# Second projection in one bank of 512 columns, its scores as row products on VectorE, the two score rows in their right roles, and a new order of work

## The reference, cut to what matters

```python
xl = (x @ W).reshape(B, N, H, F)
asrc = jnp.einsum('bnhf,hf->bnh', xl, a_src)
adst = jnp.einsum('bnhf,hf->bnh', xl, a_dst)
e = jax.nn.leaky_relu(asrc[:, :, None, :] + adst[:, None, :, :], NEG_SLOPE)
e = jnp.where(mask[..., None], e, NEG_INF)
attn = jax.nn.softmax(e, axis=1)
out = jnp.einsum('bsdh,bshf->bdhf', attn, xl)
h = jax.nn.elu(gat_layer(x, mask, W1, att_src1, att_dst1, b1, concat=True))
h = gat_layer(h, mask, W2, att_src2, att_dst2, b2, concat=False)
```

## Time and profile before

| | us |
|---|---|
| median of 3 runs (3081.1 to 3087.44) | 3084.61 |
| the profiled execution, its own time | 3083.84 |
| its span, first to last instruction | 3082.1 |
| TensorE busy | 2976.9 (97%) |
| VectorE busy | 2480.0 (80%) |
| ScalarE busy | 2319.9 (75%) |
| GpSimd busy | 2263.2 (73%) |

### The profile page before, as it was taken

The page is one execution under the profiler, slowest core; times in us unless marked ns, Lnnn a source line. Parts: engine busy times, 40 slices in busy tenths (PEclk is TensorE's granted clock), DMA queues, the critical chain, the costliest instruction groups (busy, mean ns, idle before and its releaser), DMA issues. The chain is left out here.

```text
span 3082.1 us, 79166 instructions
## 1 busy us (share of the span) xinstructions
PE 2976.9 (97%) x21040; PEld 2746.1 (89%) x21040; DVE 2480.0 (80%) x8101; ACT 2319.9 (75%) x6433; POOL 2263.2 (73%) x3214
## 2 busy tenths in 40 slices
PE   7899999999999999999999999999999999999974
PEld 5789999999999999999999999999999999999964
DVE  3578888888888888888888888888888888888852
ACT  2567787778877788777787778877788777787752
POOL 3467777777777777777777777777777777777753
PEclk6999999999999999999999999999999999999985
DMA  5123333333333333333333333333333333333332
GB/s 195 34 69 123 117 119 122 108 124 118 119 123 106 125 117 119 122 109 122 118 119 121 108 122 120 120 118 112 121 120 119 118 110 122 120 120 119 96 107 93
DMA packets 205558, 355.71 MB, mean 115 GB/s; under 512 B 51904, under 2 KB 117568, under 8 KB 188736
## 3 DMA queue, kind: packets, MB, share of 16 engines
q1 hardware_dynamic: 205120, 350.66, 34.8%
HBM read 314.93 MB, written 35.59 MB: 114 GB/s over the span
## 5 line engine op out<-in xcount | busy, mean ns | idle before, releaser
L1454 POOL TENSOR_SCALAR rs<-mv,rs 128x1 f32<-128x1 f32 x512 | 357.6, 698 | 109.2 <-POOL rs L1451 108.8
L997 ACT ACTIVATE eT<-eT,tc 128x128 f32<-128x128 f32 x1024 | 314.1, 389 | 161.3 <-POOL eT L1534 161.3
L432 PE MATMUL bank_b<-w_hi,hT_hi 128*128 128x344 f32 x1536 | 419.8, 328 | 5.6 <-DVE g L1277 3.8
L432 PE MATMUL bank_c<-w_hi,g_hi 128*128 128x258 f32 x2048 | 414.1, 283 | 4.7 <-DVE x L1204 4.7
L432 PE MATMUL bank_c<-w_lo,g_hi 128*128 128x258 f32 x2048 | 414.5, 284 | 0.0
L432 PE MATMUL bank_b<-w_lo,hT_hi 128*128 128x344 f32 x1536 | 408.2, 320 | 0.0
L1329 DVE CUSTOM_DVE_ANT_0 t_all_L<-t_all_L,mask 128x128 f32<-128x128 f32 x1024 | 368.6, 413 | 27.0 <-DMA t_all_L<-t_dram_L 26.5
L432 PE MATMUL bank_b<-w_hi,hT_lo 128*128 128x344 f32 x1536 | 357.0, 327 | 0.0
L432 PE MATMUL bank_c<-w_hi,g_lo 128*128 128x258 f32 x2048 | 351.8, 284 | 0.0
L432 PE MATMUL bank_e<-w_hi,hT_hi 128*128 128x264 f32 x1024 | 341.1, 347 | 5.5 <-DVE out_sb L1372 5.4
L1540 POOL TENSOR_TENSOR eT<-eT,shift_all 128x512 f32<-128x512 f32 x256 | 331.1, 1294 | 4.6 <-ACT eT L997 4.4
(11 more groups left out here) (158 smaller groups left out, 8577.5 us busy)
## 6 DMA issues: line engine op xcount, KB each, us to landing
shift_all<-shift_dram SPq DMA_DIRECT2D x128, 1024.0 KB, 5.3
t_all_L<-t_dram_L SPq DMA_DIRECT2D x128, 512.0 KB, 3.7
x_in<-in_x SPq DMA_DIRECT2D x128, 256.0 KB, 2.6
t_all_L1a<-t_dram_L1a SPq DMA_DIRECT2D x128, 256.0 KB, 3.2
out<-out_sb SPq DMA_DIRECT2D x128, 256.0 KB, 3.1
t_all_L<-t_dram_L SPq DMA_DIRECT2D x256, 64.0 KB, 3.1
adj_in<-in_adj SPq DMA_DIRECT2D x128, 64.0 KB, 3.0
t_dram_L1a<-t_rows_L1a SPq DMA_DIRECT2D x512, 0.5 KB
```

What stands on the lines that cost most here:

```text
L432: last = mm(bank[:, 0:width], a[:, c * P:(c + 1) * P], w[:, c, b * width:(b + 1) * width], start=(first and c == chunks[0] and n == 0), st ...
L997: last = activation(eT[:, k, :], eT[:, k, :], ACT.Prelu, bias=tc3[:, k:k + 1], alpha=SLOPE)
L1454: ts(b, mv[layer][:, 0:1], r, -1.0, ALU.mult, ALU.mult).then_inc(sem(f"rs_made{layer}"), 1)
```

## The change

It makes the second projection 512 columns wide in one bank (24 matmuls for a graph where there were 48), leaves out the turned copies of W2 and the matmuls on them before the loop, and takes the two scores of L1b as `score_columns` does for L0 and L2, straight from PSUM: `columns_L1b`. The rows of the two score vectors are loaded to all partitions (`att_dst2` takes the place that is the bias of a row, `att_src2` the one that is turned to a row). The transpose of L1b's probabilities goes to bank 1. All five lists of stages are in another order, and some stages move by one turn: `project_L1b_first_high` and `masked_L1a`, `leaky_L1a` (a turn earlier for their graph), `leaky_L3_first`, both `shift_L3`, `residual_L0`, `stats_1`, `stats_0`, `make_mask_loop` (earlier), `make_mask` (later). SKEW is 11.

```diff
-SKEW = 12
+SKEW = 11
-        w2_hi = sb("w2_hi", [P, C1, E2], F32R)
+        w2_hi = sb("w2_hi", [P, C1, D], F32R)
-        product = sb("product", [P, 4, D], BF16)
+        product = sb("product", [P, 2, D], BF16)
...
+        with_columns = [n for n, (kind, _) in enumerate(w_chunks) if kind != "w2"]
+        units = [(n, q) for n in with_columns for q in range(2 if n < C else 1)]
...
+                             (s_row[4][:], att_dst2), (t_row[4][:], att_src2),
...
@@ SyncE, each turn
                 load(t.graph(0))
-                store(t.graph(12))
-                spread_L2(t.graph(7))
+                send_shift_L3(t.graph(10))
+                send_L1b(t.graph(5))
+                spread_shift_L3(t.graph(10))
                 send_L0(t.later_graph(2))
+                spread_L1b(t.graph(5))
                 spread_L0(t.later_graph(2))
-                send_L1b(t.graph(5))
-                send_shift_L3(t.graph(10))
-                spread_L1b(t.graph(5))
-                spread_shift_L3(t.graph(10))
                 send_L1a(t.graph(3))
+                send_L3(t.graph(9))
                 spread_L1a(t.graph(3))
-                send_L3(t.graph(9))
+                spread_L3(t.graph(9))
                 send_L2(t.graph(6))
-                spread_L3(t.graph(9))
+                store(t.graph(11))
+                spread_L2(t.graph(6))
@@ TensorE
             for u in range(len(units)):
                 columns_of_weights(u)
-                if units[u] == (C + 1, 0):
+                if units[u] == (C - 1, 1):
                     pe.wait_ge(sem("L0_exp"), 1)
...
             def project_L1b(g, products, chunks, first, final):
-                return project({0: bank_c[:, 0, :], 1: bank_c[:, 1, :]}, B2, chunks, products, first, final)
+                return project({0: bank_c[:, 0, :]}, D, chunks, products, first, final)
...
-                project_L1b_first_high(t, t.graph(5))
                 project_L1b_first_low(t, t.graph(5))
+                turn_mask_L3(t, t.graph(10))
+                turn_h3(t, t.graph(9))
                 project_L1b_last(t, t.graph(5))
                 turn_mask(t, t.graph(3))
-                turn_h3(t, t.graph(9))
+                product_L3_last(t, t.graph(11))
                 turn_prob_L1a(t, t.graph(4))
-                product_L3_last(t, t.graph(11))
+                product_L3_first(t, t.graph(11))
                 turn_h1(t, t.graph(3))
-                turn_mask_L3(t, t.graph(10))
                 product_L1a_last(t, t.graph(4))
                 product_L1a_first(t, t.graph(4))
-                product_L3_first(t, t.graph(11))
...
                 product_L0(t, t.later_graph(2))
-                project_L3_first(t, t.graph(9))
+                project_L1b_first_high(t, t.graph(4))
@@ ScalarE, each turn, after
+                values_L3(10), exp_L3_last(11), exp_L1a(4), copy_mask_L3(10), hT_hi_L3(9), norm_0(2),
+                exp_L3_first(11), norm_1(3), pT_L1a(4), copy_mask(3), hT_hi_L1a(3), leaky_L2(7), elu_last(4),
+                exp_L2(7), g_hi_last(4), elu_first(4), pT_L2(7), norm_2(6), g_hi_first(4), leaky_L1b(5),
+                leaky_L0(2), exp_L1b(5), exp_L0(2), leaky_L3_first(10), pT_L1b(5), pT_L0(2),
+                leaky_L3_last(10), norm_3(8), leaky_L1a(3)
@@ VectorE
+            def score_columns(layer, src, g):
+                dve.wait_ge(sem(f"st_made{last_columns[0]}"), columns_issued[last_columns[0]])
...
+                    last = nc.vector.tensor_tensor_reduce(product[:, i, :], src, row[layer][:], 1.0, first,
+                                                          ALU.mult, ALU.add, col)
+            def columns_L1b(g):
+                if g.live:
+                    dve.wait_ge(sem("L1b_xl"), g.made())
+                    dve.wait_ge(sem("L1b_leaky"), g.made(1))
+                    dve.wait_ge(sem("L1b_rows"), g.made(1))
+                    score_columns(4, bank_c[:, 0, :], g)
...
-                    nc.vector.transpose(t_rows["L1b"][:], bank_c[:, 1, B2 - Q:B2]).then_inc(sem("L1b_rows"), 1)
+                    nc.vector.transpose(t_rows["L1b"][:], targets[4][:]).then_inc(sem("L1b_rows"), 1)
...
@@ VectorE, each turn, after
+                moments_1(3), sources_L3(10), targets_L3(10), stats_2(6), most_L1a(4), most_L3_last(10),
+                most_L3_first(10), moments_2(6), recip_L1a(4), most_leaky_L3(10), rows_shift_L3(10),
+                hT_lo_L3(9), moments_3(8), columns_L1b(5), columns_L0(2), rows_L1b(5), moments_0(1),
+                rows_L0(2), hT_lo_L1a(3), most_L2(7), recip_L3(11), result_L3(11), elu_L1a_last(4),
+                recip_L2(7), rows_L1a(3), values_L1b(5), stats_0(0), rows_L3(9), elu_L1a_first(4),
+                columns_L2(6), most_L1b(5), residual_L2(7), most_L0(2), recip_L1b(5), rows_L2(6),
+                stats_3(7), g_lo_first(4), recip_L0(2), values_L1a(3), residual_L1b(5), residual_L0(2),
+                stats_1(2)
@@ GpSimd, each turn, after
+                scale_1(3), make_mask(2), prob_L1a(4), masked_L2(7), scale_2(6), scale_0(1),
+                make_mask_loop(2), scale_3(8), out_L3(11), g_lo_last(4), masked_L1b(5), masked_L0(2),
+                masked_L3_first(10), masked_L3_last(10), shift_L3_first(10), masked_L1a(3), shift_L3_last(10)
```

More of the change, by code:

```diff
@@ L219, in build @@
         w_cols = {"w1": D1, "w2": D, "w3": D}
-        wt_dram = {"w1": w1_turned, "w2": w2_turned, "w3": w3_turned}
-        w_loads = [sum(16 * (2 + (m < C)) for m in range(n % WR, n + 1, WR)) for n in range(ALL)]
+        wt_dram = {"w1": w1_turned, "w3": w3_turned}
+        w_loads = [sum(16 * (1 + len([u for u, _ in units if u == m])) for m in range(n % WR, n + 1, WR)) for n in range(ALL)]
         first = Graph(0, G)
@@ L237, in stage_weights @@
                         .then_inc(sem(f"w_in{n % WR}"), 16)
-                    for q in range(w_cols[kind] // D):
+                    for q in range(len([u for u, _ in units if u == n])):
                         sp.dma_start(turned[n % WR][q], wt_dram[kind][c][:, q * D:(q + 1) * D])\
@@ L310, in send_L1b @@
             def send_L1b(g):
-                send_one("L1b", g, Q - 3)
+                send_one("L1b", g, 0)
             def spread_L1b(g):
@@ L400, in columns_of_weights @@
                         last = mm(e[:, at // 2:2 * H1:H1], wt, attc1[:, at, :], start=(at % 2 == 0), stop=(at % 2 == 1))
-                    elif kind == "w2":
-                        last = mm(e[:, 8:12], wt, attc2[:, b, :], start=(b == 0), stop=(b == C - 1))
                     else:
@@ L884, in pT_L1b @@
                 if g.live:
-                    pT_one("L1b", g, bank_c[:, 0, 0:P])
+                    pT_one("L1b", g, bank_c[:, 1, 0:P])
             def leaky_L2(g):
@@ L1136, in moments_3, with columns_of_h @@
                 moments(3, g)
-            def score_columns(layer, g):
+            columns_issued = {0: 0, 2: 0, 4: 0}
+            last_columns = [0]
+            def score_columns(layer, src, g):
+                dve.wait_ge(sem(f"st_made{last_columns[0]}"), columns_issued[last_columns[0]])
+                columns_issued[layer] += 1
+                last_columns[0] = layer
+                for i, (row, first, col) in enumerate(((s_row, first_of[layer], st[layer][:]),
+                                                       (t_row, 0.0, targets[layer][:, 0:1]))):
+                    last = nc.vector.tensor_tensor_reduce(product[:, i, :], src, row[layer][:], 1.0, first,
+                                                          ALU.mult, ALU.add, col)
+                last.then_inc(sem(f"st_made{layer}"), 1)
+            def columns_of_h(layer, g):
                 dve.wait_ge(sem(f"h_made{layer}"), g.made())
@@ L1142, in score_columns @@
                 dve.wait_ge(sem(f"L{layer}_rows"), g.made(1))
-                for i, (row, first, col) in enumerate(((s_row, first_of[layer], st[layer][:]),
-                                                       (t_row, 0.0, targets[layer][:, 0:1]))):
-                    last = nc.vector.tensor_tensor_reduce(product[:, layer + i, :], h[layer][:], row[layer][:], 1.0, first,
-                                                          ALU.mult, ALU.add, col)
-                last.then_inc(sem(f"st_made{layer}"), 1)
+                score_columns(layer, h[layer][:], g)
+            def columns_L1b(g):
[4 more added lines that the diff above has]
+                    score_columns(4, bank_c[:, 0, :], g)
             def columns_L0(g):
                 if g.live:
-                    score_columns(0, g)
+                    columns_of_h(0, g)
             def columns_L2(g):
                 if g.live:
-                    score_columns(2, g)
+                    columns_of_h(2, g)
             def rows_one(layer, g):
```

222 lines of the change are left out of this document (108 added, 114 removed).

## The result

The changed kernel takes 3179.14 us (median of 4 runs, 3171.54 to 3196.98) where the one before takes 3082.86 on the same chip: ratio 1.0319, 95% interval 1.0274 to 1.0365. Forecast were 3034 and a range up to 3070.

A forecast was written before the change was run, and what follows sets the result against it. TensorE's own work was taken to set the steady turn of 22.62 us. The projection's 42 us plus 8.5 before the loop made 50.5 less than the median 3084.61: 3034 us, range 2998 to 3070.

The forecast's parts named there:

- The order at nothing: Steady turn on all engines: the reordered stages were laid beside TensorE's turn and expected to cost 0 us.
- ScalarE's tail: Leaky, norm_3 and values_L3 ahead of turn_h3: least room, ending about 22.8 us for turn_h3 due at 23.2.
- the sign named for it: The prediction would be wrong if TensorE idled regularly ahead of turn_h3, project_L1a_last or turn_exp_L1b.
- a wait takes a part: Rival: ScalarE's tail or L3's masks late by 0.25 us a turn, 30 us back, 3064 us; chance 0.17.
- VectorE hidden: L1b's two score products on VectorE add 1.3 us a turn, 20.5 busy in 22.27, and still fit.
- VectorE becomes the bound: Rival: VectorE keeps its idle time and adds 1.3 us, turn 23.9 us, 3232 us (smaller form 3100); chance 0.09.
- Maxima and neighbours: VectorE beside GpSimd: slow L3 maximum may go, up to 0.7 us a turn back; new products expected without contention.
- The width: Second projection on TensorE: 24 matmuls of 512 columns at 0.227 us, 5.45 us, gaining 0.35 a turn, 42 us.
- fixed rest: TensorE's fp32r matmuls: 0.0133 us a matmul beyond 0.417 ns a column, taken as the same at every width.
- the change of width does nothing: Rival: projection cost goes by columns alone, 0.045 us a turn, 5 us, and with the setup 3071; chance 0.04.
- Before the loop: Setup without W2's turned columns: the loop starts 8.5 us earlier (5 to 13.6), first line 450 at 51 to 52.
- The drain: End of the run, turn set by L3's way across all engines: 0 gained, with 10 us either way.

The follow-up runs named there:

- e2_tail: Changed kernel with sources_L3 and targets_L3 moved to the end of the turn before, between residual_L1b and residual_L0: 3091.63 us, 1.0031 to the kernel before.
- e14_less_outside: Changed kernel with four 512-column matmuls left out of project_L1b_first_high, ahead of turn_h3: 3151.18 us, 1.0211 to the kernel before.
- e15_less_inside: Changed kernel with four 512-column matmuls left out of project_L1b_last, behind turn_h3: 3124.53 us, 1.0133 to the kernel before.
- e3_l2: Changed kernel with pT_L2 ahead of elu_first on ScalarE and product_L2 ahead of project_L3_last_low on TensorE: 3162.88 us, 1.0275 to the kernel before.
- e4_both: Changed kernel with the edits of both e2_tail and e3_l2: 3080.62 us, 1.0000 to the kernel before.
- e5_noprod: Changed kernel, its own order, with columns_L1b's two products summed over only the first 8 of 512 columns: 3175.51 us, 1.0307 to the kernel before.
- e1_old_order: Changed kernel's computation with all stage lists, SKEW and bank waits of before the change: 3222.63 us, 1.0455 to the kernel before.
- e6_oldnoprod: e1_old_order with columns_L1b's two products summed over the first 8 columns only: 3079.56 us, 0.9998 to the kernel before.
- e11_halves: e8_pT_first with the second projection as 48 matmuls of 256 columns in place of 24 of 512: 3059.72 us, 0.9924 to the kernel before.
- e8_pT_first: e4_both with pT_L1b ahead of leaky_L3_first on ScalarE: 3064.69 us, 0.995 to the kernel before.
- e9_send_L0: e8_pT_first with send_L0 ahead of the 1 MB spread_shift_L3 on SyncE: 3073.08 us, 0.9968 to the kernel before.
- e12_exp_first: e11_halves with exp_L1b ahead of leaky_L0 on ScalarE: 3065.64 us, 0.9941 to the kernel before.
- e7_spread_last: e4_both with send_L1b, send_L0, spread_L1b and spread_L0 ahead of the 1 MB spread_shift_L3 on SyncE: 3229.17 us, 1.0481 to the kernel before.

## Why the prediction was wrong, point by point

**The order at nothing: this is the step that failed.** "Least room has ScalarE's tail", "0.14 us to spare before, and it held", "so I cost the order at nothing". The place was right, and the sign named for it came: TensorE idles regularly ahead of `turn_h3`. The reading was not. The 0.14 us are no room: they stand between `xa` and `turn_h3` in every turn before and in every turn after, also where TensorE waits. The margin was nothing, and a ring of 22.61 us already stood beside TensorE's own work, which the prediction took as the only thing that sets the turn. I had laid the lists once, from t = 0 of TensorE, with the distances from start to start of the trace before. That leaves out what only a loop shows: `turn_h3` had moved ahead of 2.8 us of projection (half of it, 12 of the 24 matmuls, and not the "two thirds" of the text), `project_L3_first` had moved in behind it with 1.47, and `residual_L0` and `stats_1` still stood ahead of VectorE's `sources_L3` and `targets_L3`. So what `xa` waits for ends at the earliest 17.9 us of TensorE plus 5.2 of VectorE and ScalarE after the last `turn_h3`. Summed once around, this is 23.06, more than the turn. Three runs show it: e2_tail (one half of the ring shortened: 88 us back), e14_less_outside and e15_less_inside (the other half). I also missed that `norm_2` waits for `product_L2` of the graph before, which had become later by `project_L3_last_low`; mending it gave 0.4% alone (e3_l2), which is within the noise of the changed kernel, and a clear 11 us on e2_tail (e4_both).

**The rival "a wait takes a part"** named this wait and priced it at 0.25 us a turn, 3064; the mean turn came 1.1 us over that of before, and 1.4 over the 22.27 of the forecast, of which 0.15 is the width. Its price had been a guess about lateness, and a ring isn't late once, it adds in every turn.

**VectorE hidden: right for the changed kernel.** Forecast were 0.65 us a product and 20.5 us busy a turn; measured 0.668 and 0.687 (the two groups below) and 2081.3 / 2400 x 23.71 = 20.56. e5_noprod shows no cost there that can be told from the noise. The rival "VectorE becomes the bound" gave 23.9 us a turn, near the 23.71 measured, but by another mechanism; its own came true in the old order, where e1_old_order took 3222.63 for its 3232 and e6_oldnoprod gives all of it back. "Hidden" depended on the order: nothing that can be measured, 4.6% and 0.7% for the same two instructions.

**Maxima and neighbours.** The groups of VectorE by shape (count, busy, mean ns, idle before):

```profile
L1343 DVE CUSTOM_DVE_ANT_0 t_all_L<-t_all_L,mask 128x128 f32<-128x128 f32 x1024 | 238.5, 295 | 5.1 <-DMA t_all_L<-t_dram_L 5.1
...
L1147 DVE CUSTOM_DVE_ANT_0 product<-bank_c,t_row 128x512 bf16<-128x512 f32 x128 | 87.9, 687 | 0.0
L1147 DVE CUSTOM_DVE_ANT_0 product<-bank_c,s_row 128x512 bf16<-128x512 f32 x128 | 85.6, 668 | 4.6 <-PE bank_c L432 4.1
...
L1306 DVE TENSOR_TENSOR g_lo<-g,g_hi 128x512 fp32r<-128x512 f32 x128 | 141.0, 1102 | 0.0
```

The maxima went from 413 to 295 ns, 0.94 us a turn back, more than the "up to 0.7" of the text: before, 244 of the 1024 ran beside GpSimd's line 1517 and took 709 ns in the mean, now none does. But `g_lo`, 0.69 us before (0.71 in the mean of 128), now takes 1.10: in 116 of the 128 it runs beside GpSimd's masks of L3, and it holds up the ring's VectorE part. GpSimd's timeline at the `g_lo` that ran from 1517.89 for 1.15 us:

```profile
1516.19 2.30 POOL L1549 TENSOR_TENSOR eT<-shift_all,mask_flat_turned 128x512 f32<-128x512 f32 x2
1518.77 1.40 POOL L1555 TENSOR_TENSOR eT<-eT,shift_all 128x512 f32<-128x512 f32 x1 [0.28 <-ACT eT L991]
```

It overlaps the two masks of line 1549 until 1518.49. Before, it mostly ran beside a GpSimd instruction on one column. The new products overlapped a GpSimd instruction in 162 of 256 cases and none took more than 0.69 us. This fits the Trainium skill (SBUF — State Buffer, section Who interferes with whom), by which a VectorE instruction with two inputs in SBUF contends with a GpSimd instruction that reads SBUF, and one with at most one does not: `g_lo` reads two tiles of SBUF, the new products read PSUM and one tile.

**The width: a term of the sum that was mis-sized.** Forecast were 0.227 us a matmul, 5.45 a graph and 0.35 us gained; the timeline of the changed kernel gives:

```profile
1501.24 0.40 PE L432 MATMUL bank_c<-w_lo,g_hi 128*128 128x512 f32 x1
...
1503.57 0.39 PE L432 MATMUL bank_c<-w_hi,g_lo 128*128 128x512 f32 x1
1503.81 0.23 PE L450 MATMUL bank_a<-identb,mask_loop 128*128 128x128 bf16 x1
```

10 steps from 1501.24 to 1503.57 are 0.233 each, the upper end: 5.60 us, 0.20 gained, 24 us for my 42. The "fixed rest" of 13 ns isn't there. The slope had been taken between 258 and 344 columns, and 258 cost what 264 cost; from 264 (0.1209) to 344 (0.1567) it is 0.448 ns a column, which gives 0.232 for 512. Halving the bank again (e11_halves) costs nothing that can be measured, so of the edit's gain most was leaving the 258. The rival "the change of width does nothing", with a cost that goes by columns alone, had the nearer mechanism; what it lacked is that step. The Trainium skill (TensorE: Matmul & The Clock Gate, section Back-to-back issue gap) gives N / 2.4 + 2.5 ns for a matmul by itself, 0.216 us for 512 columns; this stream has 0.233, so its rule doesn't carry over.

**Before the loop: the size right, by two errors that cancel.** 8.5 us were forecast, 8.1 came, 51.7 for "51 to 52". W3's columns began later than I had it (40.75 for 38.2), for a turned chunk that was still on its way, and ended at 47.9 for 45.1. The loop then followed 3.8 us behind them, where before it was 6.1, so that the sum is right is partly luck. The first of W3's units:

```profile
40.75 1.87 PE L405 MATMUL bank_b<-attc,g 128*128 128x4 f32 x8 [4.17 <-DMA g<-in_w_turned]
```

**The drain** gained 10.8 us, just over my "10 either way"; no run isolates why.

**What the change was worth with its order mended.** e8_pT_first gains 20 us of span on the kernel before: 8.8 before the loop (first line 450 at 51.0), 6.8 behind the last, and only 4 in 127 turns. The floor fell by 0.27 us (22.61 to 22.34), and both floors are lengths of the ring; the long turns took nearly all of it. What makes each of them long stays open: e9_send_L0 and e12_exp_first each removed a wait and gained nothing.

## What to carry to other kernels

When stages are reordered in a software pipeline, sum each loop once around across engines, from an instruction back to the same one a turn later, at every buffer that is reused; an engine with 97% busy time hides a loop of the same length, and it shows when anything moves. A gap between two engines that is the same in every turn is no slack but the hand-over: here 0.14 us in 106 of 106. Whether added work is hidden is a property of the place in the order, not of the engine's idle share. And to tell a loop from a busy engine, leave the same work out once inside and once outside of it.

## What the runs showed of the hardware that was not expected

- fp32r matmuls of 256, 258, 264, 344 and 512 columns start 0.118, 0.1208, 0.1209, 0.1567 and 0.233 us apart at the full granted clock: no fixed part that a merge of two would save, and a small step between 256 and 258.
- A VectorE subtraction of two SBUF tiles of 512 columns took 0.66 to 0.69 us with no GpSimd instruction beside it (3 cases), 0.69 beside one on a single column, and 1.14 in the mean of 116 beside GpSimd's multiplications of two tiles.
- A TensorE instruction that waited for ScalarE's copy started 0.14 us behind the copy's end, in all 101 steady turns of the changed kernel.
- A 1 MB transfer issued one send and two small reads later (e7_spread_last against e4_both) cost 4.8% of the whole time, more than any other single move tried here; from issue to landing it took 7.1 us in the median, 4.8 in the changed kernel.
